# Turned blocks of one head pair dealt out one by one behind the next pair's projections, in a graph-attention kernel

## The reference

```python
h = jnp.maximum(_layernorm(x), 0.0)
q = h @ wq.T + bq;  k = h @ wk.T + bk;  v = h @ wv.T + bv
q2 = (q @ wiq.T + biq).reshape(N, H, D).transpose(1, 0, 2)
k2 = (k @ wik.T + bik).reshape(N, H, D).transpose(1, 0, 2)
v2 = (v @ wiv.T + biv).reshape(N, H, D).transpose(1, 0, 2)
scores = jnp.einsum('hnd,hmd->hnm', q2, k2) / 8 + mask[None]
attn = jax.nn.softmax(scores, axis=-1)
out = jnp.einsum('hnm,hmd->hnd', attn, v2).transpose(1, 0, 2).reshape(N, 1024)
return x + out @ wo.T + bo
```

## Time and profile before

| | |
|---|---|
| median of 3 runs | 287.85 us (287.68 to 288.86) |
| the profiled execution | 287.73 us |
| its span, first to last instruction | 285.9 us |
| TensorE busy | 279.7 us, 98% of the span |
| VectorE, ScalarE, GpSimd busy | 178.2, 157.2, 152.0 us |
| chain that ended last | TensorE 96% of the span |
| mean granted clock of TensorE | 0.999 of full |

### The profile page before, as it was taken

The page is one execution under the profiler, slowest core; times in us unless marked ns, Lnnn a source line. Parts: engine busy times, 40 slices in busy tenths (PEclk is TensorE's granted clock), DMA queues, the critical chain, the costliest instruction groups (busy, mean ns, idle before and its releaser), DMA issues.

```text
span 285.9 us, 5992 instructions
## 1 busy us (share of the span) xinstructions
PE 279.7 (98%) x2346; PEld 264.3 (92%) x2346; DVE 178.2 (62%) x443; ACT 157.2 (55%) x287; POOL 152.0 (53%) x157
## 2 busy tenths in 40 slices
PE   6899999999999999999999999999999999999996
PEld 2799998888899999999999999999999999898885
DVE  3999878787667743334564877666667566754121
ACT  2986443282148434323442697977878787985000
POOL 6461444646346664655102597957658494786100
PEclk9999999999999999999999999999999999999999
DMA  7978965653942434555957213506132231231032
GB/s 241 327 266 268 335 195 179 223 176 115 390 158 76 150 82 138 147 147 130 252 131 171 76 58 93 148 4 148 44 106 76 73 88 64 77 87 62 0 147 73
DMA packets 16366, 40.90 MB, mean 143 GB/s; under 512 B 3769, under 2 KB 5714, under 8 KB 16338
## 3 DMA queue, kind: packets, MB, share of 16 engines
q1 hardware_dynamic: 13746, 38.53, 42.9%
q0 software_dynamic: 2016, 1.21, 1.8%
q10 hardware_dynamic: 576, 0.79, 0.8%
HBM read 37.71 MB, written 2.81 MB: 142 GB/s over the span
## 4 chain that ended last, share of the span: by engine, by line
PE 96%; DMA 1%; DVE 1%; ACT 0%; POOL 0%; issue 0%
PE banks L1132 23%; PE banks L1005 18%; PE banks L1007 18%; PE banks L1006 18%; PE banks L1198 6%; PE banks L1151 4%; PE banks L1180 3%; PE banks L1246 3%; DMA x_sb<-in_x 1%; PE banks L1054 1%; DVE stats L816 1%; PE banks L1094 1%; PE banks L1097 0%; PE banks L1084 0%; ACT x_sb L613 0%; POOL rstd L468 0%
## 5 line engine op out<-in xcount | busy, mean ns | idle before, releaser
L510 POOL DMA_INDIRECT cells<-value,cell x51 | 54.2, 1063 | 52.3 <-DMA cells<-value,cell 37.0
L564 ACT ACTIVATE w_hi<-raw 128x1024 fp32r<-128x1024 f32 x50 | 51.7, 1054 | 22.7 <-PE banks L1007 19.1
L1007 PE MATMUL banks<-a_lo,w_hi 128*128 128x384 f32 x184 | 61.5, 334 | 0.0
L1005 PE MATMUL banks<-a_hi,w_hi 128*128 128x384 f32 x184 | 61.5, 334 | 0.0
L1006 PE MATMUL banks<-a_hi,w_lo 128*128 128x384 f32 x184 | 61.5, 334 | 0.0
L483 POOL TENSOR_TENSOR w_lo<-raw,w_hi 128x1024 fp32r<-128x1024 f32 x15 | 36.7, 2451 | 40.7 <-ACT w_hi L564 40.7
L863 DVE TENSOR_TENSOR w_lo<-raw,w_hi 128x1024 fp32r<-128x1024 f32 x35 | 42.2, 1228 | 9.9 <-ACT w_hi L564 9.9
L1005 PEld LDWEIGHTS banks<-a_hi,w_hi 128*128 128x128 f32 x184 | 34.5, 188 | 0.0
L1006 PEld LDWEIGHTS banks<-a_hi,w_lo 128*128 128x128 f32 x184 | 34.5, 188 | 0.0
L1007 PEld LDWEIGHTS banks<-a_lo,w_hi 128*128 128x128 f32 x184 | 34.5, 188 | 0.0
L675 ACT ACTIVATE prob<-prob,neg_max 128x384 f32<-128x384 f32 x48 | 29.0, 606 | 5.2 <-DVE neg_max L921 5.2
(11 more groups left out here) (153 smaller groups left out, 577.9 us busy)
## 6 DMA issues: line engine op xcount, KB each, us to landing
raw<-in_slabs SPq DMA_DIRECT2D x40, 512.0 KB, 3.5
raw<-in_slabs SPq DMA_DIRECT2D x32, 256.0 KB, 4.1
prob<-key_rows SPq DMA_DIRECT2D x8, 256.0 KB, 3.9
x_sb<-in_x SPq DMA_DIRECT2D x3, 512.0 KB, 5.1
out_y<-x_sb SPq DMA_DIRECT2D x5, 256.0 KB, 2.1
cells<-prob SPq DMA_DIRECT2D x2, 576.0 KB, 7.9
cells<-value,cell POOLq DMA_INDIRECT x51, 4.0
work<-key_rows SPq DMA_DIRECT2D x3, 256.0 KB, 5.3
```

Of the source, the lines that this page charges most:

```text
L510: nc.gpsimd.indirect_dma_start(out=cells[c][:, :], out_offset=bass.IndirectOffsetOnAxis(ap=cell[:, t:t + 1], axis=0), in_=value[:, t:t + 1 ...
L564: nc.scalar.activation(split_place(s)[0], raw_place(s), ACT.Copy).then_inc(slab_hi, 1)
L1005: nc.tensor.matmul(psum, w[0], a[0], start=first, stop=False)
L1007: return nc.tensor.matmul(psum, w[0], a[1], start=False, stop=last)
```

## The change

One piece of the order on TensorE is written in another way; no instruction is removed, and none with work is added. In each iteration j from 1 to 6 the projections of pair j + 1 now run to step 21 before the turns begin (TURNS_FROM = 22, and not 30). Then one block (two transposes) and one projection step (two matmuls) alternate, 18 times: block 0, step 22, block 1, step 23, and so on to block 17, step 39. Steps 40 to 47 and the values follow as before. The waits of the three thirds stand before their first blocks. Since every step is now a `pair_steps` call of its own, each of the 18 asks for the low part of its slab again.

```diff
+TURNS_FROM = 22
...
-            def turn(pair, m):
-
-                at, j = turn_place(pair, m), pair + 1
+            def turn_waits(pair, m):
+
+                j = pair + 1
...
-                for b in (2 * m, 2 * m + 1):
-                    for n in range(NT):
-                        for high in range(2):
...
+            def turn(pair, m):
+
+                turn_waits(pair, m)
+                for i in range(2 * NT):
+                    turn_block(pair, m, i)
+
+            def turn_block(pair, m, i):
+
+                at, b, n = turn_place(pair, m), 2 * m + i // NT, i % NT
+                for high in range(2):
+                    own = slice(high * D, (high + 1) * D)
+                    to = (b % 2 * NT + n) * D
+                    columns = prob[own, pair % 2, n, b, :, :].rearrange("p x d -> p (x d)")
+                    mm = nc.tensor.transpose(bank[at + high][:, to:to + D], columns, ident[own, own])
+                    if n == NT - 1:
+                        mm.then_inc((pt_done, pt_done_high)[high], 1)
...
-                pair_steps(j + 1, cuts[2], 30)
-                for m in range(NT):
-                    turn(j - 1, m)
-                pair_steps(j + 1, 30, 48)
+                pair_steps(j + 1, cuts[2], TURNS_FROM)
+                for i in range(6 * NT):
+                    m = i // (2 * NT)
+                    if i % (2 * NT) == 0:
+                        turn_waits(j - 1, m)
+                    turn_block(j - 1, m, i % (2 * NT))
+                    pair_steps(j + 1, TURNS_FROM + i, TURNS_FROM + i + 1)
+                pair_steps(j + 1, TURNS_FROM + 6 * NT, 48)
```

## The result

The changed kernel takes **293.19 us** (median of 4 runs, 293.07 to 293.31), the kernel before 287.83 in the same comparison: the ratio is 1.0185, with a 95% interval of 1.0169 to 1.0200. That is 5.4 us slower; 293.9 were forecast, within 291.2 to 297.0. The profiled execution took 293.15 us with a span of 291.3, against 287.73 and 285.9: the whole difference lies inside the span.

A forecast was written before the change was run, and what follows sets the result against it. TensorE's own issue was taken as the bound; 17 dearer blocks add 1.0 us per iteration, +6.0 in six, so 287.73 + 6.0 = 293.7, and with 0.12 for the median 293.9 us; range 291.2 to 297.0.

The forecast's parts named there:

- TensorE's own issue is the bound: TensorE, busy 98% of the span: time added to or taken from its list enters the result one for one.
- Term 2: Run of transposes on TensorE: a block followed by a block costs 0.062 us, one followed by a projection 0.12 us.
- the rival named there: Named in the experiments: a price of the change from transpose to product that grows with the product's columns; no chance given.
- Term 3: The 18 dealt blocks: each now costs 0.12 us, so +1.0 us per iteration and +6.0 us in six.
- The cheaper rival: Dealt blocks: 0.12 is partly start-up after a long run, a single block costs 0.08 to 0.11; 289.3 to 292.5, chance 0.07.
- The bounds: Block price limits: columns only, -2.7 us in all; also waiting for its own load, +12.6 us in all.
- The 0.040 of the columns alone: Dealt blocks, faster rival: projection weights fetched early, so a block costs only its columns, 0.040 us; 285.1 us, chance 0.05.
- The 0.18 of a block that also waits for its own load: Dealt blocks, upper bound: 0.062 for its own load on top of 0.12; up to 300.3 us, dearer rival's chance 0.10.
- Term 4: Waits of the moved blocks and of the values: all cost nothing, with about 1 us in hand at pt_lo.
- The rule of the Trainium skill: Projection weight loads: columns divided by 1.2, 107 ns for 128 columns, so a block costs 0.107 and the sum is +4.6.

The follow-up runs named there:

- the groups: Changed kernel with the blocks dealt in groups of 2, 3 or 6 behind as many projection steps, from step 22: 290.59, 289.74 and 288.63 us.
- three widths: Changed kernel with the weights of projection steps 22 to 39 cut from 128 columns to 72 or 96: 288.18 and 290.35 us; uncut 293.19 us.
- the last experiment: Changed kernel with each block and its step issued half by half, transpose then projection for rows 0 to 63, then 64 to 127: 293.19 us against 288.28.

## Why the prediction was right

**TensorE's own issue is the bound** (part on what bounds the kernel): right. The six iterations are 0.90 us longer each, and span and time are 5.4 us longer; nothing absorbed them.

**Term 2, two prices for a block:** right, and now shown apart. In the groups the blocks that a block follows cost 0.055 (the first) and 0.062, and only the last one is dear, 0.12 as read. What makes it dear is the load of the next projection's weights, which shrinks with its columns; that was argued from one pair of load rows before, and is now measured at three widths, save for the rival named there that no run tests.

**Term 3, the price for a run of one:** right in kind, a little high in size. I took the 0.12 us of the end of a run for a block alone. The end of a run does cost that, in runs of 18, 6, 3 and 2; a block alone costs 0.115. 17 x (0.115 - 0.062) = 0.90 us per iteration and 5.4 in six, where 17 x 0.058 = 1.0 and 6.0 stood. This is nearly all of the 0.7 by which the forecast was too slow. The cheaper rival, that a single block costs less than the end of a run, was right in its direction, but by 0.005 us and not by the 0.01 to 0.04 that it asked for, and not for its reason, the length of the run: at the end of a run of two the price is the full 0.12. In the load rows the difference looks so: the transposes' load comes 0.13 behind that of the projection (168.17 to 168.30) and not 0.12 as I expected, but the transposes start 0.15 behind their load, where a projection starts 0.17 to 0.18 behind its own.

**The bounds:** neither was reached. The 0.040 of the columns alone (285.1 us) needs a load fetched a whole step early, and the loads show that this doesn't happen. The 0.18 of a block that also waits for its own load doesn't either: the transposes' load has the 384 columns of the projection before as cover, in all 108 blocks.

**Term 4, the waits:** right. No row of a transpose, projection or value has idle time. The part said to be nearest, pt_lo of the last third in iteration 2:

```profile
188.29 0.96 DVE L936 TENSOR_TENSOR pt_lo<-banks,pt_hi 128x768 fp32r<-128x768 f32 x1 [0.77 <-ACT pt_hi L687]
...
188.78 0.34 PE L1207 MATMUL banks<-pt_hi,v 64*128 64x384 f32 x2
...
190.52 0.33 PE L1207 MATMUL banks<-pt_lo,v 64*128 64x384 f32 x2
```

It is done at 189.25 us and first read at 190.52, the eleventh step of the values (I had it needed two steps sooner): 1.3 us were in hand. I had forecast its end at 188.4 and the ninth step at 189.4, and they came at 189.25 and 190.17. Both forecasts were 0.8 to 0.9 early, since I left out that iteration 1 already pushes all of iteration 2 back by 0.9. The same shift was missing on both sides, so the time in hand came out nearly right all the same. ScalarE and VectorE now wait between the thirds, pt_hi 0.8 us at a time, and nobody waits for them.

**The rule of the Trainium skill**, as the prediction applied it, would have given 292.4 and the rows 293.9; 293.2 lies between. For a block that has a 128-column load of a projection behind it the measured price is 0.115, above the 0.107 that the page's rule made of it and under my 0.12.

## What to carry to other kernels

Ask of each small matmul not only what covers its own weight load, but whose load it has to cover: behind 64 moving columns most of a load of 128 product columns stands exposed (a block costs 0.115 us, where its moving columns alone would make 0.040 by the prediction's estimate), while 384 hide all of it. Small matmuls belong together, in runs, with one long one before them; dealing them out between long ones gives each a load to expose, here 0.05 to 0.06 us for every place where a long one follows a short one. When a list is reordered at constant work, count these places before and after: that count times one row's price gave the whole result, here within 0.7 us.

## What the runs showed that I had not expected

In the last experiment the transpose of the second half stands in the list behind the first half's projection. By the records both transposes start within 0.01 us of one another (168.10, x2), ahead of both projections (168.13, x2), as they do where the list has them so. So between the two halves of the rows the order of the kernel's text isn't the order of the starts, and what I wrote at the beginning, that an engine runs its list in its order, doesn't hold there as it stands. Whether TensorE or an earlier stage of the build does this was not tried.

In a run the transposes go on with 0.062 us a block, although as many columns are loaded for them (128) as for a projection, behind which a block costs 0.115 to 0.12. The rows of the loads differ too: 0.14 us for the 128 columns of a transpose, as long as for 72 columns of a projection, and 0.19 for 128. What differs is the kind (transpose mode against reduced float32 products); which part of it makes the load shorter stays open.
